# Half of the first token chunk's feed-forward part placed inside the last attention step

## The reference

```python
qkv = einsum('bsd,ed->bse', x, w_qkv) + b_qkv          # 16 heads of 32
attn = softmax(q k^T / sqrt(32) + causal mask)         # per head, 1024 x 1024
y = layernorm(x + einsum('bsd,ed->bse', attn v, w_out) + b_out)
hidden = relu(einsum('bsd,hd->bsh', y, sign(up_w)) * up_scale)       # 2048 wide
out = layernorm(y + einsum('bsh,dh->bsd', hidden, sign(down_w)) * down_scale * output_scale)
```

## Time and profile before

| | |
|---|---|
| median of 3 runs | 775.22 us (774.33 to 776.11) |
| profiled execution, its time | 774.34 us |
| its span in the trace | 772.6 us |
| mean granted TensorE clock | 0.991 |
| TensorE busy | 722.7 us (94%) |
| VectorE / ScalarE / GpSimd busy | 450.5 / 317.2 / 354.4 us |
| chain that ended last | PE 71%, DVE 19%, issue 3%, DMA 3%, POOL 2% |

### The profile page before, as it was taken

The page is one execution under the profiler, slowest core; times in us unless marked ns, Lnnn a source line. Parts: engine busy times, 40 slices in busy tenths (PEclk is TensorE's granted clock), DMA queues, the critical chain, the costliest instruction groups (busy, mean ns, idle before and its releaser), DMA issues.

```text
span 772.6 us, 11683 instructions
## 1 busy us (share of the span) xinstructions
PE 722.7 (94%) x4032; PEld 505.2 (65%) x4032; DVE 450.5 (58%) x1086; ACT 317.2 (41%) x631; POOL 354.4 (46%) x487
## 2 busy tenths in 40 slices
PE   6899999999999999999979889999999999999993
PEld 4788665655656556565544544788778787878882
DVE  4176495785967859678567751633294339334515
ACT  5211365654655546555546565432232222122210
POOL 4461467394673946739423502632353235223333
PEclk9999999999999999999999999999999999999998
DMA  6976464435544355452677331313012001000101
GB/s 231 296 208 177 110 174 124 136 105 163 150 132 132 108 157 148 115 133 88 174 206 261 109 123 58 120 32 119 14 41 95 28 1 41 15 1 12 44 1 54
DMA packets 44619, 85.71 MB, mean 111 GB/s; under 512 B 4880, under 2 KB 13584, under 8 KB 44432
## 3 DMA queue, kind: packets, MB, share of 16 engines
q1 hardware_dynamic: 35536, 79.72, 34.2%
q10 hardware_dynamic: 9024, 5.24, 2.4%
HBM read 55.33 MB, written 29.36 MB: 110 GB/s over the span
## 4 chain that ended last, share of the span: by engine, by line
PE 71%; DVE 19%; issue 3%; DMA 3%; POOL 2%; ACT 2%; SPq 0%; ACTq 0%; POOLq 0%
PE ps_heads L1045 9%; PE ps_proj L1087 7%; DVE heads_sb L835 7%; PE ps_proj L947 7%; PE ps_score L1104 6%; PE ps_unit L1063 6%; PE ps_unit L1087 5%; PE ps_sum L1039 5%; DVE maxes L813 5%; PE ps_unit L983 4%; PE ps_heads L1104 3%; PE ps_unit L1015 3%; PE ps_sum L1104 3%; PE ps_score L1015 2%; PE ps_score L983 2%
## 5 line engine op out<-in xcount | busy, mean ns | idle before, releaser
L655 POOL TENSOR_TENSOR hid_low<-hid_raw,hid_high 128x512 fp32r<-128x512 f32 x64 | 85.1, 1330 | 175.0 <-DVE hid_high L886 171.9
L711 ACT ACTIVATE probs<-ps_unit 128x512 f32<-128x512 f32 (+3 forms) x216 | 101.9, 490 | 88.4 <-PE ps_unit L1015 85.0
L619 POOL TENSOR_SCALAR_AFFINE_SELECT probs<-probs 128x128 f32<-128x128 f32 x256 | 73.1, 298 | 113.0 <-ACT probs L711 108.9
L711 ACT ACTIVATE probs<-ps_score 128x512 f32<-128x512 f32 (+3 forms) x155 | 75.2, 498 | 77.0 <-PE ps_score L1015 75.6
L886 DVE CAST hid_high<-hid_raw 128x512 fp32r<-128x512 f32 x64 | 27.1, 424 | 125.4 <-ACT hid_raw L766 125.2
L809 DVE CUSTOM_DVE_ANT_0 ps_unit<-ps_unit,causal 128x512 f32<-128x512 f32 (+3 forms) x162 | 80.1, 511 | 32.5 <-PE ps_unit L983 31.5
L1045 PE MATMUL ps_heads<-probs,v_rows 128*32 128x512 f32 (+3 forms) x768 | 80.3, 502 | 11.8 <-DVE heads_sb L837 11.8
L983 PE MATMUL ps_unit<-stack 96*128 96x512 f32 (+3 forms) x246 | 83.8, 354 | 5.7 <-DVE maxes L809 2.5
L1015 PE MATMUL ps_unit<-stack 98*128 98x512 f32 (+2 forms) x216 | 78.4, 366 | 4.1 <-DVE maxes L809 4.0
L613 POOL TENSOR_TENSOR parts<-qk_full,parts 128x512 fp32r<-128x512 f32 x32 | 41.3, 1289 | 64.7 <-ACT parts L690 64.4
L835 DVE RECIPROCAL heads_sb<-ps_sum 128x128 f32<-128x128 f32 x64 | 60.8, 950 | 9.2 <-PE ps_sum L1039 9.2
(11 more groups left out here) (195 smaller groups left out, 1478.0 us busy)
## 6 DMA issues: line engine op xcount, KB each, us to landing
stack<-qk_parts SPq DMA_DIRECT2D x96, 256.0 KB, 4.6
qk_parts<-parts SPq DMA_DIRECT2D x32, 512.0 KB, 2.9
v_all<-h_even ACTq DMA_DIRECT2D x16, 256.0 KB, 3.8
v_rows<-v_all SPq DMA_DIRECT2D x8, 512.0 KB, 4.3
heads_t<-heads_sb SPq DMA_DIRECT2D x16, 256.0 KB, 3.4
raw<-up_w SPq DMA_DIRECT2D x8, 512.0 KB, 3.9
x_tile<-x_rows SPq DMA_DIRECT2D x16, 256.0 KB, 5.5
raw<-down_w SPq DMA_DIRECT2D x8, 512.0 KB, 3.4
```

Of the source, the lines that this page charges most:

```text
L655: nc.gpsimd.tensor_tensor(hid[1][:, (HM * s + n) % 3, :], hid_raw[:, n % 2, :], hid[0][:, (HM * s + n) % 3, :].bitcast(FP32), ALU.subtract ...
L711: nc.scalar.activation(probs[:, (NP * s + n) % RING, 0:width], bank(what, s, n)[:, off:off + width], ACT.Exp, scale=SCALE).then_inc(s_exp, 1)
```

## The change

Chunk 0 is cut into two rounds of 256 tokens (`ROUNDS`): round 0 (tiles 0 and 1) has its 16 `up` and 16 `down` steps from slot 14 to slot 49 of the last attention step; round 1 (tiles 2 and 3) follows the last score, in chunk 0's old place but with 256 instead of 512 tokens; rounds 2 to 4 are chunks 1 to 3 as before. `attn`, `y`, `norm1` and `turn` of chunk 0 move earlier, from the end of step 6 to slot 13 of step 7. The order of the weight jobs becomes `JOBS`, and all signs are done by slot 36 of the last step. For score pieces 15 and later of the last step only two PSUM banks are left. Chunk 1's `split` to `turn` lie inside round 1. New buffers `hid0` hold round 0's hidden values. The order that each engine gets around the end of the last step, written out from the new slots:

The diff, cut to its core:

```diff
-ALONE_NORM = [[18.4, 18.41, 18.42, 18.43, 50.4, 50.41, 50.42, 50.43],
+ALONE_NORM = [[19.25, 19.26, 19.27, 19.28, 50.4, 50.41, 50.42, 50.43],
...
-NJOBS = 18
...
+ROUNDS = [(0, (0, 1)), (0, (2, 3))] + [(i, tuple(range(TT))) for i in range(1, CH)]
+TILES = [0, 2, 4, 8, 12, 16]
+FILL_FROM = 15
+JOBS = [("out", 0), ("out", 1)] + [("up", k) for k in range(4)] + [("down", 0), ("down", 1), ("up", 4), ("down", 2), ("up", 5),
+        ("down", 3), ("up", 6), ("down", 4), ("up", 7), ("down", 5), ("down", 6), ("down", 7)]
...
+    last = NP * (STEPS - 1)
+    signs = [late + 23, late + 25.5] + [late + 28.5 + 3.6 * k for k in range(4)] + [late + 43, late + 46]
+    signs += [last + at for at in (3, 6, 9.5, 13, 16.5, 20, 24, 28, 32, 36)]
     for k, at in enumerate(signs):
-        put(late + 17.2 if k < 2 else signs[k - 2] + (3 if k < 4 else 0.5), "job", 0, k)
+        put(late + 17.2 if k < 2 else signs[k - 2] + 0.5, "job", 0, k)
         put(at, "sign", 0, k)
-    last = NP * (STEPS - 1)
     put(late + 30, "fetch", 0)
     put(late + 31, "fetch_x", 0)
     put(last + 12, "fetch", 1)
-    for i in range(4):
-        put(late + 38 + 2 * i, "split", 0, i)
-        put(late + 46.5 + 1.3 * i, "bias", 0, i)
+    for i in range(TT):
+        put(late + 37.5 + 1.5 * i, "split", 0, i)
+        put(late + 40 + 1.3 * i, "bias", 0, i)
         for m in range(12):
-            put(last + 0.5 + 5.2 * i + 0.42 * m, "attn", 0, 12 * i + m)
-        put(last + 5.8 + 5.2 * i, "y", 0, i)
-        put(last + 23 + i, "norm1", 0, i)
-        put(last + 26 + 2.5 * i, "turn", 0, i)
-    put(last + 22.5, "std1", 0)
-    for i in range(CH):
-        t = FIRST_UP + 16 * i
+            put((late + 44.5, late + 47.1, last + 2.5, last + 5.5)[i] + 0.22 * m, "attn", 0, 12 * i + m)
+        put((late + 47, last + 2.2, last + 7.7, last + 8.2)[i], "y", 0, i)
+        put(last + 9 + 0.1 * i, "norm1", 0, i)
+        put((last + 10.2, last + 10.9, last + 12.6, last + 13.2)[i], "turn", 0, i)
+    put(last + 8.6, "std1", 0)
+    for r, (i, tiles) in enumerate(ROUNDS):
+        t = FIRST_UP + 16 * (r - 1)
         for m in range(HM):
-            put(t + m, "up", i, m)
-            if i < CH - 1 or m < HM - 2:
-                put(t + m + 2.5, "down", i, m)
-        if i == CH - 1:
-            for q in range(TT):
+            put(t + m if r else last + 14 + 2.05 * m, "up", r, m)
+            if r < len(ROUNDS) - 1 or m < HM - 2:
+                put(t + m + 2.5 if r else last + 18.4 + 2.05 * m, "down", r, m)
+        if r == len(ROUNDS) - 1:
+            for q in tiles:
                 put(t + 17, "finish", i, q)
-        for q in range(TT):
-            put(t + 17.55, "z", i, q)
-            put(t + 18.6 + q, "ln2", i, q)
-            put(t + 19.5 + q, "out", i, q)
-        if i + 1 < CH:
+        end = t + 17.55 if r else FIRST_UP + 2.1
+        for q in tiles:
+            put(end, "z", i, q)
+            put(end + 1.05 + q, "ln2", i, q)
+            put(end + 1.95 + q, "out", i, q)
+        if r and i + 1 < CH:
             if i:
                 put(t - 4, "fetch", i + 1)
-            put(t + 0.5, "fetch_x", i + 1)
+            put(t + 0.2, "fetch_x", i + 1)
             for q in range(TT):
-                put(t + 2.2 + 0.7 * q, "split", i + 1, q)
-                put(t + 3 + q, "bias", i + 1, q)
+                at = 2 * q if i else 2.5 * q
+                put(t + (2.2 + 0.7 * q if i else 0.3 + 0.4 * q), "split", i + 1, q)
+                put(t + (3 + q if i else 1 + q), "bias", i + 1, q)
                 for m in range(12):
-                    put(t + 5.2 + 2 * q, "attn", i + 1, 12 * q + m)
-                put(t + 6 + 2 * q, "y", i + 1, q)
-                put(t + 6.7 + 2 * q, "ln1", i + 1, q)
-                put(t + 7.4 + 2 * q, "turn", i + 1, q)
+                    put(t + (5.2 if i else 3) + at, "attn", i + 1, 12 * q + m)
+                put(t + (6 if i else 4.3) + at, "y", i + 1, q)
+                put(t + (6.7 if i else 5.1) + at, "ln1", i + 1, q)
+                put(t + (7.4 if i else 6.3) + at, "turn", i + 1, q)
...
-            may = (2, 3, 4, 5) if s == STEPS - 1 else (0, 1, 2, 3, 4)
+            may = (2, 3, 4)[n >= FILL_FROM:] if s == STEPS - 1 else (0, 1, 2, 3, 4)
...
+        def attn_bank(s, i):
+            return ps_unit[0] if s else (ps_proj, ps_proj, ps_unit[0], ps_unit[1])[i]
+        def turn_bank(s, i):
+            return ps_unit[1] if s else (ps_proj, ps_unit[0], ps_unit[1], ps_unit[0])[i]
+        def down_bank(r, i):
+            return ps_unit[i] if r == 0 else ps_down[i - 2] if r == 1 else ps_down[i]
+        def hidden(r):
+            return (hid0, hid0_raw) if r == 0 else (hid, hid_raw)
+        def tokens(r):
+            return P * len(ROUNDS[r][1])
...
-                eng.wait_ge(s_dt, TT * (steps // HM))
+                eng.wait_ge(s_dt, TILES[steps // HM])
...
-                        if n == 6:
+                    if kind == "up":
+                        if k == 4:
...
+                    if kind == "down":
+                        if k == 0:
+                            act.wait_ge(s_used, GH * ADDING)
+                            for q in range(NB):
...
-                        wait(act, s_up, HM * (s - 1))
+                        wait(act, s_up, HM * s if s > 1 else 0)
...
+                        act.wait_ge(s_score, NP * (STEPS - 1))
+                    if s == 1 and n == 0:
...
+                    if s == 0 and n == 0:
+                        dve.wait_ge(s_pv, NP * STEPS)
                     dve.wait_ge(s_dt, TT * s + n + 1)
                     wait(dve, s_o, TT * (s - 1) + n + 1)
-                    nc.vector.tensor_tensor(z_sb[:, n, :], ps_down[n][:, :], gain[:, :], ALU.mult).then_inc(s_z, 1)
+                    src = down_bank(0 if n < 2 else 1, n) if s == 0 else ps_down[n]
...
                         pe.wait_ge(s_hlo, DC * (s + 1))
                         if s == 0:
                             pe.wait_ge(s_sign, 2)
                             pe.wait_ge(s_wol, 2)
-                    if s == 0 and m == 0 and i < 2:
-                        bank_read(last_user[i])
-                    if m == 0:
-                        wait(pe, s_y, TT * s + i - (s == 0))
-                    mm = nc.tensor.matmul(ps_attn[s > 0][i % 2][:, :], turned[s % 2][xp][:, c, i * P:(i + 1) * P], wo[wp][:, c, :],
+                            pe.wait_ge(s_qk, NB * STEPS)
+                        if s == 1:
+                            pe.wait_ge(s_z, 1)
+                    if s == 0 and m == 0 and i > 1:
+                        bank_read(last_user[i - 2])
+                    if m == 0 and (s > 0 or i == 1):
+                        wait(pe, s_y, TT * s + i)
+                    mm = nc.tensor.matmul(attn_bank(s, i)[:, :], turned[s % 2][xp][:, c, i * P:(i + 1) * P], wo[wp][:, c, :],
                                           start=(m == 0), stop=(m == 11))
                     if m == 11:
                         mm.then_inc(s_at, 1)
                 if what == "turn":
                     pe.wait_ge(s_h1, TT * s + n + 1)
-                    wait(pe, s_tl, TT * s + n)
+                    if s > 0 or n == 3:
+                        pe.wait_ge(s_tl, TT * s + n if s else 2)
+                    if s == 1 and n == 0:
+                        pe.wait_ge(s_z, 2)
                     for c in range(DC):
-                        mm = nc.tensor.transpose(ps_turn2[:, c * P:(c + 1) * P], h1[s % 2][:, n, c * P:(c + 1) * P],
+                        mm = nc.tensor.transpose(turn_bank(s, n)[:, c * P:(c + 1) * P], h1[s % 2][:, n, c * P:(c + 1) * P],
                                                  ident[:, :])
                     mm.then_inc(s_tt, 1)
                 if what == "up":
+                    i, tiles = ROUNDS[s]
                     if n == 0:
-                        pe.wait_ge(s_tl, TT * (s + 1))
-                    if s == 0 and n < 2:
-                        bank_read(last_user[(5, 2)[n]])
+                        pe.wait_ge(s_tl, TILES[s + 1])
+                    if s == 0 and n == 1:
+                        bank_read(last_user[2])
                     if s == 0:
-                        pe.wait_ge(s_sign, 3 + n // 2)
+                        pe.wait_ge(s_sign, JOBS.index(("up", n // 2)) + 1)
                     wait(pe, s_hr, HM * s + n - 1)
                     for m in range(2 * DC):
-                        mm = nc.tensor.matmul(ps_up[n % 2][:, :], up_sb[n // 8][:, n % 8, m % DC, :],
-                                              turned[s % 2][m // DC][:, m % DC, :],
+                        mm = nc.tensor.matmul(ps_up[n % 2][:, 0:tokens(s)], up_sb[n // 8][:, n % 8, m % DC, :],
+                                              turned[i % 2][m // DC][:, m % DC, columns(s)],
                                               start=(m == 0), stop=(m == 2 * DC - 1))
                     mm.then_inc(s_up, 1)
                 if what == "down":
+                    i, tiles = ROUNDS[s]
                     if s == 0:
```

(28 more changed lines are left out.)

68 lines of the change are left out of this document (34 added, 34 removed).

## The result

The changed kernel took **789.30 us** (median of 4, 788.14 to 789.83) beside 775.42 of the kernel before in the same session: ratio 1.0178, 95% interval 1.0161 to 1.0196. It is slower by some 14 us. The predicted 785.0 was 4.3 us short, and the range 777 to 793 holds the result.

What follows compares the result with a forecast made beforehand. TensorE was taken as under way nearly throughout, with VectorE in every large wait and at most 9.4 us to win. New costs of 19.8 us less 9.4 gone gave +10.4 on 774.3, so 785 us, range 777 to 793.

Steps and rivals of the forecast that it cites:

- (a): Chunk 0's first y: attn matmul 12 waits for y of tile 0 behind VectorE's last maximum; 1.7 us, 0.5 to 2.5.
- (b): Chunk 0's layer norm after step 6: TensorE waits at turn 0, turn 3 and down 2; 3.9 us, 2 to 6.
- (c): Body of the last step: two score banks, relu chain and signs cost nothing, with 0 to 10 as ends.
- the rival: Scores wait for exp in the last step: two banks don't do, 16 pairs at 0.61 us, +9.8, 795 us; chance 0.11.
- (d): Hand-over after the last sum: chunk 1's first attn waits for VectorE's splits and first z; 5.8 us, 4.8 to 9.
- (e): Attn of chunk 1's tile 1 waits for y of tile 0, which shares its bank; 3.6 us, 2 to 4.5.
- Narrower matmuls: Chunk 0's up: 256 matmuls of 256 columns instead of 128 of 512; +1.3 us, bounds 0 and 2.6.
- Half clock: TensorE at 1.2 instead of 2.4 GHz behind (d) and one of (b) and (e); 3.5 us, 1.8 to 7.
- the signs come 3 to 4 slots apart; a raw load is issued two signs ahead ... nothing: Part of (c), last step: SP's store and fetch between signs wait for things long done, so no cost.
- the change doesn't come off: Rival: a late sign or load holds up or down of round 0 for a DMA, a few us, 788; chance 0.04.

Runs made afterwards that it cites:

- e10: e8 with only 8 of 128 columns done in the last four of step 6's eight normalisations, so it computes something else: 777.41 us.
- e4: The kernel before with only two PSUM banks for score pieces 15 and later of the last step: 780.95 us.
- e6: The kernel before with chunk 0's up steps as 2 x 8 matmuls of 256 columns instead of 8 of 512: 777.85 us.
- e1: The changed kernel with the fourth sign of up_w moved back from slot -8.7 to -5.2 of the last step: 785.15 us.
- e7: The changed kernel with the fourth sign of up_w and chunk 0's four splits put back where they stood before: 786.13 us.
- e8: e7 with the hand-over reordered: last four normalisations late, chunk 1's steps later, tile 1's ln2 and out of round 0 behind chunk 1's y: 777.83 us.
- e12: e8 with chunk 0's attn and y later and GpSimd's bias of tile 3 behind the last split: 774.39 us.
- e11: The kernel before with the first two maxima for step 7 moved earlier on VectorE, ahead of normalisations: 780.68 us.
- e5: The kernel before with only the four signs of up_w earlier, by 0.5, 1.5, 2.5 and 3.5 slots: 782.66 us.
- e2: The changed kernel with the last step's normalisations 4 to 7 moved on VectorE behind the layer norms of chunk 1's tiles: 786.34 us.

## Why the prediction was right, step by step

Direction, mechanism and rough size were right. That the sum came within 4.3 us is in part luck: two terms were too small by 8.8 us together, one of them held at nothing, three were too large by 2.4, and 2.7 us of the measured loss stay unexplained.

- **(a)** 1.7 forecast, 1.2 measured, at the place named. **(b)** 3.9 forecast, 3.0 measured (2.7 at turn 0, 0.3 at turn 3), with e10 showing that most of it is the layer norm's chain.
- **(c)**, nothing for the body and the two banks: right. 462 to 514 us is 51.95 us busy of 52. e4 shows what that rests on: the same two banks cost some 6 us where `up` and `down` don't lie between, with one long wait behind a root and five short ones, not sixteen as the rival had it.
- **(d)** 5.8 forecast, 5.8 measured; attn 10.8 us after the last sum where 10.6 was counted. The best term, since it is only a queue read out in order with durations of rows. One of its items was not as counted: the cast of 256 columns took 1.34 instead of 0.25 us beside GpSimd's bias, while both last splits together took 1.8.
- **(e)** 3.6 forecast, 2.6 measured; `out` 0 took 0.83 of the up to 1.44 us allowed for.
- **Narrower matmuls** +1.3 forecast; 1.1 by the spacing in e6.
- **Half clock** 3.5 new less 1.8 gone was forecast, and +5.4 was measured, in one execution of each kernel. The term took 1.75 us for (d) and as much for one of (b) and (e), by the earlier trace rows. Behind (d) and (e) together the changed kernel lost 4.5 us and e1, with the same two waits, 1.6: the price of a gap is a range, in which the 3.5 lies. The other 2.6 us stand behind (f), and those the sum had left out with it.
- **The step that failed is "the signs come 3 to 4 slots apart; a raw load is issued two signs ahead ... nothing".** It looked at the last step, where that is true, and not at the fourth sign of `up_w` in step 6, which comes 3.5 slots earlier, ahead of a load whose time SP's queue sets. This is (f), 5.1 us of waits in the changed kernel. e1 shows how much of it is the sign: put back, TensorE idles 2.9 us less and the run is some 4 us faster, while 2.2 us of waits on maxima stay. Of that rest, 1.4 us stood on maxima before too, counted as gone, which is not what happened. Its link to the steps that the change moves forward in step 6 is argued: with the splits put back (e7) the waits on maxima fall to 0.6 us, and 2.5 us stand before attn 0 instead. The rival "the change doesn't come off" named the mechanism, a late sign or load, but placed it in `up` and `down` of round 0 and gave it 0.04.

By the terms: 10.4 - 0.5 - 0.9 - 1.0 + 5.1 + 3.7 = 16.8, against 14.0 measured; the 2.7 us left open above are in it.

One sum of the prediction is wrong: with every bound at its high end it comes to 22.2 us without (c) and 32.2 with (c) at 10, not "about +25". The forecast and the range don't rest on it.

What the change is worth without its new waits, e8 and e12 answer: nothing that is sure. The filler does fill (482 to 490 us is whole), but the idle time of before was put there by VectorE's and ScalarE's chains, and each chain has its counterpart in the new place: in e12 TensorE still idles 7.3 us. Whether the kernel before would gain from the same care for the order was tried only at one place (e11), and that was a miss.

## What to carry to other kernels

When a step is moved in a hand-written order, look at every queue it passes, and for a consumer of a load at the moment its DMA lands, not only at the distance to its issue: signs up to 3.5 slots early cost 7 us by themselves. Where two parts of a kernel meet, write the slow engine's queue out and put what the next matmul needs first; here that order was worth 8 us with the same instructions. Count a gap on TensorE with the half clock behind it, as a range: 1.6 to 4.5 us behind the same two waits here. And do not read a difference of one or two us of half clock between two single profiles as the work of an edit, above all where it lies at a place that the edit leaves alone.

## What the runs showed of the hardware

- In e5 a wait of 3.0 us was followed by 17 us at 1.2 GHz, 429 to 446 us, in which TensorE was busy 15.15 us; in the earlier trace rows a gap of 4 us was followed by 3.4 us at half clock (a clock of 0.66 over 5 us). Even the same wait doesn't have one price: behind the 5.8 us at the hand-over and the 2.6 us after it half clock took 4.5 us in the changed kernel, 4.4 in e7 and 1.6 in e1. In the changed kernel the clock fell only as TensorE started again (0.96 at 523 to 524 us, 0.50 from 524); in e1 it fell in the middle of the wait (0.59 at 520 to 521 us), and it was back at 527 instead of 531. What decides it no run here shows.
- A cast of 128x256 on VectorE took 0.29 us alone (520.26) and 1.34 beside a GpSimd add of 1.71 us (522.20, above), while the two z, which read PSUM, took 0.65 each (523.98) though GpSimd worked all through them. The Trainium skill ("GPSIMD Engine Reference", "Key points") says that GpSimd shares SBUF interfaces with VectorE, with contention for instructions that read two SBUF inputs or run in a two-port mode; by that rule the split suffers and z does not, and the trace agrees: two splits took 2.83 us beside the bias in e2 and 1.28 without it. The cast reads one input; whether it runs in a two-port mode no run here shows. Nor is it always VectorE that pays: the addition of the residual to z at 525.82 in the changed kernel, with two SBUF inputs, took 0.68 us beside GpSimd as it did alone (535.51), and GpSimd's low part beside it took 1.11 instead of 0.74.
